# An adaLN transformer block on one core: the next unit's projection placed between the fourth and fifth up tile, with the chains, loads and stores that hang on it

## The chip, the cores and the metric

The kernel runs on one core of a Trainium2 chip. The metric is the device time of one execution in microseconds. A core has a matrix engine (TensorE, PE in the profile), a vector engine (VectorE, DVE), a scalar engine (ScalarE, ACT), GpSimd (POOL), and a queue that issues DMA transfers (SyncE, SP). Each runs its own instruction stream in order and waits for the others by semaphores.

## The reference

Eight sequences of 1024 tokens with 512 features go through one block:

```python
h = layernorm(x) * (1 + ca) + sa
x = x + ga * attention(h)                      # 16 heads, causal
h = layernorm(x) * (1 + cb) + sb
shared = relu(h @ shared_up.T)**2 @ shared_down.T          # 1024 hidden features
routed = sum over the 4 chosen of 32 experts of weight * (relu(h @ up.T)**2 @ down.T)
x = x + gb * (routed + shared)
```

The modulations (sa, ca, ga, sb, cb, gb) are computed from a small conditioning input. The router takes sigmoid(h @ gate.T), adds a bias, picks 4 of 8 groups and then 4 of 32 experts for each token, and gives every expert 256 places, filled in the order of the tokens.

## The kernel before

It has four stages: the first layernorm with the projections to q, k and v; the attention; the "ffn" stage (`project_programs`), which takes the output projection, the second layernorm, the router and the shared expert; and the 32 routed experts (`experts_programs`), which gather their tokens by index. All large products are fp32 made of three matmuls of two-part numbers (high x high, high x low, low x high): helper `exact`, L2191. So most operands exist as a pair, `_hi` and `_lo`: ScalarE or GpSimd makes the high part and VectorE or GpSimd the low part from it.

The ffn stage is where the change lies. It runs over 16 units of 512 tokens (`u = 2 * b + half`, `b` the sequence), each four token tiles (`UT = 4`, `PT = 3` is the last). Two neighbouring units overlap: while unit u goes through the shared expert, the next one is projected, normalised and transposed. Each engine has its own function `body(b, half, more)`, written out by hand, and its order of lines is the order of execution; there is no scheduler. In a middle unit:

- **TensorE**: router logits (L2251, L2253, L2254); up tiles 0 to 7 into four PSUM banks `ps_m0` to `ps_m3` (12 matmuls each), with the small matmuls that turn the logits back (L2234) after tile 0; `project` of the next unit, four tiles of 12 matmuls (`wo` times `o`); `places`, small matmuls that count places per expert (L2222 to L2225); down tiles 0 to 3, 24 matmuls each, in eight pairs of three. `turn` puts four transposes of one tile of the next unit (L2210) behind down tile 1 (tile 0), behind down tile 2 (tiles 1 and 2) and in the middle of down tile 3 (tile 3). The table `TURNS` holds that. A transpose waits for its modulated tile of `h2` and, through `lo_done`, for the low part of the tile two before it, because there are two banks `ps_t`. The first down tile waits for all eight low parts of the activations.
- **VectorE**: adds the logits (L2134); for each up tile n the low part `a_lo` (L2147), and behind the first six of them one of the steps 0 to 5 of `choose`, the router's selection; `attend` of the next unit: four times the gate sum (L145, L147, L149, and the statistics L151), the variance (L276 to L284), the reciprocal root (L290 to L298), four norms (L2025), and multiply and add of the last tile (L2032, L2034); then for each down tile the output (L2171 times gate, L2173 added to x) with the low parts of the transposed tiles (L1993) between; last `give_slots` (L2113 to L2128), which turns places into addresses. In unit 14 `give_slots` stands before `attend` and `places` before `project`.
- **ScalarE**: relu (L1965), square (L1949) and high part (L1953) of each up tile, the high part one tile later than its square; the sigmoid (L1958) behind tile 0; the root for the norm (L1930) behind tile 7; high parts of the transposed tiles (L1936).
- **GpSimd**: `modulate` of tiles 0 to 2 (L1873, L1875); `normalise` of the attention output two units ahead (L1884, L1887, L1889); 16 indirect DMAs that scatter the unit's tokens and weights to the experts' lists (`scatter`, L1912). In unit 14 four of the 16 come before `modulate`.
- **SP**: loads `o` (after the projection of the next unit, which frees its buffer), stores `h2`, stores the output (1 MB, after four tiles) and, when that has landed, loads `x` of the unit two ahead into the same buffer.

Unit 0 has the projection, the chain and its own table of choice steps behind it; unit 15 has no next unit. Ahead of the stage, the attention's end normalises and modulates unit 0 (L1253, L1259, L1266).

## Time and profile before

| | us |
|---|---|
| median of 3 runs | 2990.87 |
| lowest and highest | 2986.22, 2996.89 |
| span of the profiled execution | 3027.5 |
| TensorE busy | 2895.4 (96%) |
| VectorE busy | 2179.3 (72%) |
| ScalarE busy | 1341.6 (44%) |
| GpSimd busy | 1833.5 (61%) |

The profile is of one execution. Its page gives busy time by engine and the costliest groups of instructions; the trace behind it can be asked for the time line of an engine, for the waits (who waited, at which line, for whom, how long in all), and for the busy time and granted clock of stretches. In a time line a bracket at a row's end is the idle time before the instruction and what ended it. The ffn stage begins at 1709.0 us and ends at 2717.9 us. The gate matmul L2254 of each ffn unit marks where I cut the units: unit 1 begins at 1779.30, unit 14 at 2598.40, unit 15 at 2665.20.

### The profile page before, as it was taken

Reading aid. Unit: us, or ns where it says so; the run is one execution under the profiler, and the core shown is the slowest. Engines: PE = TensorE matmul, PEld = TensorE weight load, DVE = VectorE, ACT = ScalarE, POOL = GpSimd, SP = SyncE. Lnnn points to the kernel's source line nnn. Section 1 sums busy time; section 2 is a strip of 40 time slices with the busy share of each in tenths; the row PEclk is TensorE's granted clock in tenths of the full one; section 3 lists DMA queues with packets and bytes.
Section 4 is the critical chain, followed back from the end, with each engine's and each line's share of the span. In section 5 each row is a group of like instructions: output and inputs, shape, how many; then the busy total and the mean of one; then the engine's idle time right before and its main releaser. Section 6 shows DMA issues by size and latency. Waiting matters only on the chain.

```text
span 3027.5 us, 49806 instructions
## 1 busy us (share of the span) xinstructions
PE 2895.4 (96%) x16480; PEld 2168.3 (72%) x16480; DVE 2179.3 (72%) x5344; ACT 1341.6 (44%) x2436; POOL 1833.5 (61%) x1077
## 2 busy tenths in 40 slices
PE   8999999999999999999999989999999999989997
PEld 5788888766666666666666677777777787767775
DVE  6555555678787878787877687777777787756664
ACT  2222222156666666666666522233222333226664
POOL 1233222278888888888886256766565666655664
PEclk9999999999999999999999999999999999999998
DMA  7655555756655665566555333332322322238996
GB/s 240 211 187 201 187 180 180 233 114 136 137 124 115 138 138 121 115 139 140 119 117 160 107 97 93 94 112 74 103 79 93 102 85 81 73 107 222 239 245 118
DMA packets 281948, 420.53 MB, mean 139 GB/s; under 512 B 48463, under 2 KB 132687, under 8 KB 281742
## 3 DMA queue, kind: packets, MB, share of 16 engines
q1 hardware_dynamic: 259214, 384.22, 44.9%
q0 software_dynamic: 22528, 33.72, 5.8%
q8 instruction: 109, 1.79, 0.3%
q14 instruction: 97, 0.79, 0.1%
HBM read 263.38 MB, written 153.01 MB: 138 GB/s over the span
## 4 chain that ended last, share of the span: by engine, by line
PE 53%; DVE 14%; POOL 14%; issue 8%; ACT 4%; DMA 4%; another core or an unknown queue 2%; DVEq 1%; POOLq 0%; SPq 0%; ACTq 0%
PE qkv_ps_m L840 12%; PE ffn_ps_m L2191 11%; POOL att_gathered L1105 6%; PE qkv_ps_m L844 6%; POOL att_pt L1098 5%; PE att_ps_o L1330 5%; PE att_ps_p L1386 4%; PE att_ps_s L1304 4%; DMA out<-exp_y,exp_tok_add 2%; PE exp_ps_u L1607 2%; PE exp_ps_y L1623 1%; PE att_ps_s L1361 1%; DVE ffn_att L147 1%; DVE ffn_x L149 1%
## 5 line engine op out<-in xcount | busy, mean ns | idle before, releaser
L247 DVE CUSTOM_DVE_ANT_0 att_ps_s<-att_ps_s,att_causal 128x512 f32<-128x512 f32 (+1 forms) x992 | 469.3, 502 | 175.5 <-PE att_ps_s L1304 171.3
L1166 ACT ACTIVATE att_pt<-att_ps_p 128x512 f32<-128x512 f32 (+1 forms) x1024 | 524.5, 589 | 143.6 <-PE att_ps_p L1389 110.2
L1304 PE MATMUL att_ps_s<-att_ks,att_qs 96*128 96x512 f32 x1488 | 513.4, 373 | 2.2 <-DVE att_lower L253 0.6
L1386 PE MATMUL att_ps_p<-att_qs,att_ks 98*128 98x512 f32 (+3 forms) x1536 | 498.5, 364 | 9.3 <-ACT att_pt L1166 8.0
L1098 POOL TENSOR_TENSOR att_pt<-att_pt 128x1024 f32<-128x1024 f32 (+2 forms) x153 | 331.1, 2164 | 166.6 <-PE att_ps_o L1330 144.8
L1105 POOL TENSOR_TENSOR att_gathered<-att_gathered,att_pt 128x2048 f32<-128x2048 f32 (+1 forms) x92 | 388.1, 4218 | 7.2
L1912 POOL DMA_INDIRECT slot_info<-ffn_info,ffn_slot x256 | 275.9, 1078 | 119.3 <-issue 76.5
L253 DVE TENSOR_REDUCE att_lower<-att_ps_s 128x1 f32<-128x512 f32 x496 | 339.2, 684 | 7.4 <-PE att_ps_s L1304 7.4
L1386 PEld LDWEIGHTS att_ps_p<-att_qs,att_ks 98*128 98x128 f32 x1536 | 272.6, 191 | 82.1 <-issue 34.7
L1304 PEld LDWEIGHTS att_ps_s<-att_ks,att_qs 96*128 96x128 f32 x1488 | 275.7, 191 | 73.3 <-DVE att_rowmax L247 27.7
L577 POOL TENSOR_TENSOR qkv_x<-qkv_x,qkv_mod 128x512 f32<-128x512 f32 x60 | 83.4, 1391 | 371.5 <-DVE qkv_x L671 371.5
L1330 PE MATMUL att_ps_o<-att_pt,att_vs 128*32 128x512 f32 (+3 forms) x3072 | 267.6, 489 | 0.0
L1873 POOL TENSOR_TENSOR ffn_h<-ffn_h,ffn_mod 128x512 f32<-128x512 f32 x45 | 70.6, 1569 | 242.1 <-DVE ffn_h L2025 242.1
L2191 PE MATMUL ffn_ps_m<-ffn_dn_hi,ffn_a_hi 128*128 128x512 f32 x512 | 208.7, 408 | 5.8 <-ACT ffn_relu L1965 3.3
L2191 PE MATMUL ffn_ps_m<-ffn_hT_hi,ffn_up_hi_first 128*128 128x512 f32 x512 | 202.1, 395 | 3.8 <-issue 3.8
L1330 PEld LDWEIGHTS att_ps_o<-att_pt,att_vs 128*32 128x32 f32 x3072 | 90.1, 109 | 158.0 <-issue 117.2
L2191 PE MATMUL ffn_ps_m<-ffn_dn_hi,ffn_a_lo 128*128 128x512 f32 x512 | 203.1, 397 | 0.0
L2191 PE MATMUL ffn_ps_m<-ffn_dn_lo,ffn_a_hi 128*128 128x512 f32 x512 | 202.9, 396 | 0.0
L840 PE MATMUL qkv_ps_m<-qkv_hT_hi,qkv_w_hi 128*128 128x512 f32 x512 | 201.3, 393 | 1.4 <-DVE qkv_hT_lo L676 1.4
L2191 PE MATMUL ffn_ps_m<-ffn_hT_lo,ffn_up_hi_first 128*128 128x512 f32 x512 | 200.2, 391 | 1.1 <-issue 1.1
L840 PE MATMUL qkv_ps_m<-qkv_hT_hi,qkv_w_lo 128*128 128x512 f32 x512 | 200.5, 392 | 0.0
L2191 PE MATMUL ffn_ps_m<-ffn_hT_hi,ffn_up_lo_first 128*128 128x512 f32 x512 | 200.2, 391 | 0.2 <-issue 0.2
(311 smaller groups left out, 6718.8 us busy)
## 6 DMA issues: line engine op xcount, KB each, us to landing
att_qs<-qk_parts SPq DMA_DIRECT2D x96, 512.0 KB, 6.8
att_ks<-qk_parts SPq DMA_DIRECT2D x96, 512.0 KB, 12.7
qk_parts<-qkv_out_hi SPq DMA_DIRECT2D x128, 256.0 KB, 2.2
qk_parts<-qkv_out_lo SPq DMA_DIRECT2D x128, 256.0 KB, 2.4
qkv_x<-x SPq DMA_DIRECT2D x16, 1024.0 KB, 5.6
v_rows<-qkv_out_v SPq DMA_DIRECT2D x64, 256.0 KB, 2.3
att_vs<-v_rows SPq DMA_DIRECT2D x32, 512.0 KB, 16.1
o_parts<-att_o SPq DMA_DIRECT2D x64, 256.0 KB, 7.9
```

Of the source, the lines that this page charges most:

```text
L247: dve.tensor_tensor_reduce(part, part, self.causal[:, UNIT - (c1 - c0):UNIT], scale=1.0, scalar=MASKED, op0=ALU.add, op1=ALU.max, accum_ou ...
L253: dve.reduce_max(under[:, low:low + 1], part, axis=AX.X).then_inc(self.max_done, 1)
L840: last = pe.matmul(ps_m[n % BANKS][:, :], w_part[:, k, (n % NG) * P:(n % NG + 1) * P], h_part[:, k, :], start=k == 0 and a + c == 0, stop= ...
L844: last = pe.matmul(ps_m[n % BANKS][:, :], h_part[:, k, t * P:(t + 1) * P], (w_hi, w_lo)[c][2][:, k, :], start=k == 0 and a + c == 0, stop= ...
L1098: pool.tensor_tensor(into, into, tile(c)[:, :, col:UNIT], ALU.add).then_inc(add_done, 1)
L1105: pool.tensor_tensor(into, into, tile(c)[:, :, col:UNIT], ALU.add).then_inc(add_done, 1)
L1166: act.activation(tile(c)[:, h, col:UNIT], ps_p[(NPROB * prev.g + n) % NP][:, col:UNIT], ACT.Exp, scale=float(HD) ** -0.5).then_inc(exp_don ...
L1304: pe.matmul(bank("s", cur.g, i)[:, 0:c1 - c0], qs[cur.slot][0:STACK, h, t * P:(t + 1) * P], ks[cur.slot][0:STACK, h, c0:c1], start=True, s ...
L1330: last = pe.matmul(ps_o[h * HD:(h + 1) * HD, col:UNIT], vs[group.slot][:, kt, h * HD:(h + 1) * HD], tile(c)[:, h, col:UNIT], start=kt == 0 ...
L1386: last = pe.matmul(part[:, i * (UNIT - col):(i + 1) * (UNIT - col)], ks[prev.slot][:, h + i, kt * P:(kt + 1) * P], qs[prev.slot][:, h + i, ...
L1912: pool.indirect_dma_start(info_dram[:, :], bass.IndirectOffsetOnAxis(slot[half][:, j:j + 1].bitcast(U32), 0), info[half][:, j, :], None, b ...
L2191: last = pe.matmul(bank, a[m], c[n], start=i + j == 0, stop=i + 1 == len(pairs) and j == 2)
```

## The change

For units 1 to 14 the projection of the next unit moves from behind up tile 7 to between up tiles 3 and 4, and what hangs on it moves along: on VectorE the gate sums and the variance stand before `a_lo` 4, the reciprocal root and the norms before `a_lo` 6, and the choice steps at 0, 1, 2, 4 and 7 (the last two together); `give_slots` stands before the outputs instead of behind them. ScalarE makes the high parts 3 and 4 directly behind their squares and takes the root behind tile 4. The first down tile waits for `a_lo` pair by pair. GpSimd modulates all four tiles. Transposes 0 and 1 both stand behind down tile 1. Unit 14 loses its special order, and its scatter is one run. Outputs are stored, and x loaded, in two halves. Ahead of the stage the 12 vector operations that normalise and modulate unit 0 become 8 with two arithmetic steps in each; the rest of the diff that is left out here renumbers semaphore counts.

```diff
         PT = UT - 1
-        TURNS = ((), (0,), (1, 2), ())
-        SCATTERED_AHEAD = TOPK
+        FIRST_TURNS, TURNS = ((), (0,), (1, 2), ()), ((), (0, 1), (2,), ())
+        PAIR = UT // 2
+        AT_ONCE = (RING - 1, RING)
         CHOSEN_AHEAD, PLACED_AHEAD = {0: (0, 1), 1: (2,), 2: (3,), 3: (4, 5)}, 4
         DOWN_AT = {0: 0, 1: 1, 3: 2, 4: 3}
         FIRST_CHOICE = {1: (1,), 5: (2,), 7: (3, 4, 5)}
+        CHOICE = {0: (0,), 1: (1,), 2: (2,), 4: (3,), 7: (4, 5)}
...
+            def load_x(b, half, t0, t1):
+                src = x[bass.ds(b, 1), half * UNIT + t0 * P:half * UNIT + t1 * P, :]
+                sp.dma_start(x_sb[half][:, t0:t1, :], src.rearrange("o (t p) d -> p (o t) d", p=P)).then_inc(x_in[half], 16)
+
+            def store_out(u, half, t0, t1):
+                sp.wait_ge(out_done, CREDIT + UT * u + t1)
+                dst = out[bass.ds(u * UNIT + t0 * P, (t1 - t0) * P), :]
+                sp.dma_start(dst.rearrange("(t p) d -> p t d", p=P), x_sb[half][:, t0:t1, :]).then_inc(x_out[half], 16)
...
-                sp.wait_ge(out_done, CREDIT + UT * (u + 1))
-                dst = out[bass.ds(u * UNIT, UNIT), :]
-                sp.dma_start(dst.rearrange("(t p) d -> p t d", p=P), x_sb[half][:, :, :]).then_inc(x_out[half], 16)
-                if not (isinstance(b, int) and b == LAST):
-                    sp.wait_ge(x_out[half], CREDIT + 16 * (b + 1))
-                    load_x(b + 1, half)
+                store_out(u, half, 0, PAIR)
+                sp.wait_ge(x_out[half], CREDIT + 32 * b + 16)
+                if b < LAST:
+                    load_x(b + 1, half, 0, PAIR)
+                store_out(u, half, PAIR, UT)
+                if b < LAST:
+                    sp.wait_ge(x_out[half], CREDIT + 32 * (b + 1))
+                    sp.wait_ge(x_in[half], CREDIT + 32 * (b + 1))
+                    load_x(b + 1, half, PAIR, UT)
...
-            def modulate(b, half):
-                u = b * HALVES + half
-                for t in range(PT):
-                    pool.wait_ge(norm_done, CREDIT + UT * u + t + 1)
+            def modulate(u):
+                for t in range(UT):
+                    pool.wait_ge(norm_done, CREDIT + UT * (u - 1) + t + 1)
                     ht = h2[:, t, :]
                     pool.tensor_tensor(ht, ht, mod[:, 1, :], ALU.mult).then_inc(mul_done, 1)
-                    pool.wait_ge(mul_done, CREDIT + PT * u + t + 1)
+                    pool.wait_ge(mul_done, CREDIT + UT * u + t + 1)
                     pool.tensor_tensor(ht, ht, mod[:, 2, :], ALU.add).then_inc(h_done, 1)
...
-                if u == UNITS - 2:
-                    scatter(u, half, 0, SCATTERED_AHEAD)
                 if more:
-                    modulate(*((b, 1) if half == 0 else (b + 1, 0)))
-                if half == 0 and not (isinstance(b, int) and b == LAST) or half == 1 and more:
+                    modulate(u + 1)
+                if b < LAST:
                     normalise(u + 2)
-                scatter(u, half, SCATTERED_AHEAD if u == UNITS - 2 else 0, UT * TOPK)
+                scatter(u, half)
...
-                    if n:
+                    if n and not (u and more and n - 1 in AT_ONCE):
                         high(n - 1)
                     square(n)
                     if n == 0 and u and more:
                         scores()
                     if u == 0 and n in DOWN_AT:
                         high_weights(NW_UP + DOWN_AT[n], NW_UP + DOWN_AT[n] + 1)
+                    if u and more and n in AT_ONCE:
+                        high(n)
+                    if u and more and n == RING:
+                        root(u + 1)
                 high(UP - 1)
+                if u == 0:
+                    root(1)
                 if more:
-                    root(u + 1)
                     turn(u + 1)
...
-            def attend(b, half):
+            def gate_sums(b, half):
 
                 u = b * HALVES + half
-                own = CREDIT + LINKS * u
                 xs = x_sb[half]
-                dve.wait_ge(x_in[half], CREDIT + 16 * (b + 1))
                 dve.wait_ge(mod_in, CREDIT + 48 * (b + 2))
                 for t in range(UT):
+                    if t == 0:
+                        dve.wait_ge(x_in[half], CREDIT + (32 * b if b else 16))
+                    if t == PAIR:
+                        dve.wait_ge(x_in[half], CREDIT + 32 * b + 16)
                     last = late.gate_sum(dve, u, t, ps_m[t % RING], att, bo_sb, mod, xs, stats, LINKS * u)
                 last.then_inc(dve_own, 1)
                 late.variance(dve, LINKS * u, stats, mv, tmp)
+
+            def norms(b, half):
+
+                u = b * HALVES + half
                 late.deviation(dve, u, LINKS * u, mv, std, rstd, tmp)
-                own += 2 * UT + 1 + STAT_LINKS + ROOT_LINKS
                 dve.wait_ge(tr_done, CREDIT + UT * u)
                 dve.wait_ge(h2_out, CREDIT + 16 * u)
                 for t in range(UT):
-                    last = dve.tensor_scalar(h2[:, t, :], xs[:, t, :], mv[:, t, 0:1], rstd[:, t:t + 1],
-                                             ALU.subtract, ALU.mult)
-                    if t < PT:
-                        last.then_inc(norm_done, 1)
-
-                last.then_inc(dve_own, 1)
-                dve.wait_ge(dve_own, own + 1)
-                dve.tensor_tensor(h2[:, PT, :], h2[:, PT, :], mod[:, 1, :], ALU.mult).then_inc(dve_own, 1)
-                dve.wait_ge(dve_own, own + 2)
-                dve.tensor_tensor(h2[:, PT, :], h2[:, PT, :], mod[:, 2, :], ALU.add).then_inc(norm_done, 1)
+                    dve.tensor_scalar(h2[:, t, :], x_sb[half][:, t, :], mv[:, t, 0:1], rstd[:, t:t + 1],
+                                      ALU.subtract, ALU.mult).then_inc(norm_done, 1)
...
+                after = (b, 1) if half == 0 else (b + 1, 0)
                 for n in range(UP):
                     if u == 0 and n == 2:
                         late.last_invert(LastGroup(GROUPS - 1), 1)
+                    if u and more and n == RING:
+                        gate_sums(*after)
+                    if u and more and n == RING + 2:
+                        norms(*after)
                     if not more:
...
-                    for step in FIRST_CHOICE.get(n, ()) if u == 0 else (n,) if more else ():
+                    for step in (FIRST_CHOICE if u == 0 else CHOICE if more else {}).get(n, ()):
                         choose(u, step)
-                if u == UNITS - 2:
+                if u == 0:
+                    gate_sums(*after)
+                    norms(*after)
+                elif more:
                     give_slots(u, half)
-                if more:
-                    attend(*((b, 1) if half == 0 else (b + 1, 0)))
...
-                        for t2 in TURNS[t]:
+                        for t2 in (TURNS if u else FIRST_TURNS)[t]:
                             low_turned(u + 1, t2)
-                if u < UNITS - 2:
+                if u == 0:
                     give_slots(u, half)
...
-                if t < PT:
-                    pe.wait_ge(h_done, CREDIT + PT * u + t + 1)
-                else:
-                    pe.wait_ge(norm_done, CREDIT + UT * (u + 1))
+                pe.wait_ge(h_done, CREDIT + UT * u + t + 1)
...
+                after = (b, 1) if half == 0 else (b + 1, 0)
                 for n in range(UP):
+                    if u and more and n == RING:
+                        project(*after, lambda t: pe.wait_ge(relu_done, CREDIT + UP * u + t + 1))
                     if n < RING:
                         pe.wait_ge(fin_done, CREDIT + UT * (u - 1) + n + 1)
+                    elif u and more:
+                        pe.wait_ge(att_done, CREDIT + UT * (u + 1) + n - RING + 1)
                     else:
                         pe.wait_ge(relu_done, CREDIT + UP * u + n - RING + 1)
                     cols = slice(n * P, (n + 1) * P)
...
-                if u == UNITS - 2:
+                if first:
+                    project(*after, lambda t: pe.wait_ge(relu_done, CREDIT + UP * u + UP - RING + t + 1))
+                if more:
                     places(u)
-                if more:
-                    project(*((b, 1) if half == 0 else (b + 1, 0)), lambda t: pe.wait_ge(relu_done, CREDIT + UP * u + UP - RING + t + 1))
-                if u < UNITS - 2:
-                    places(u)
-
-                if more:
-                    pe.wait_ge(alo_done, CREDIT + UP * (u + 1))
                 if first:
+                    pe.wait_ge(alo_done, CREDIT + UP)
                     pe.wait_ge(w_lo_done, CREDIT + NW)
                 for t in range(UT):
-                    if more:
-                        pe.wait_ge(att_done, CREDIT + UT * (u + 1) + t + 1)
+                    if first:
+                        pe.wait_ge(att_done, CREDIT + UT + t + 1)
                     else:
-                        pe.wait_ge(relu_done, CREDIT + UP * (u + 1))
+                        pe.wait_ge(relu_done, CREDIT + UP * u + RING + t + 1)
                     cols = slice(t * P, (t + 1) * P)
 
                     def before_pair(n):
                         if more and t == PT and 2 * n == UP:
                             turn(u + 1, PT)
-                        if not more and t == 0:
+                        if not first and t == 0:
                             pe.wait_ge(alo_done, CREDIT + UP * u + n + 1)
 
                     exact(ps_m[t % RING][:, :], [((a_hi[:, n, cols], a_lo[:, n, cols]), (dn_hi[:, n, :], dn_lo[:, n, :]))
                                                  for n in range(UP)], before_pair).then_inc(down_done, 1)
                     if more:
-                        for t2 in TURNS[t]:
+                        for t2 in (TURNS if u else FIRST_TURNS)[t]:
```

On TensorE, in a middle unit, the order before, from the end of up tile 3 to the first down tile (within a tile one of its 12 matmuls stands for all; `wo` and `o` mark the projection, `dn` the down tiles):

```order
L2191 MATMUL ffn_ps_m3<-ffn_hT_hi,ffn_up_lo_first 128x512
L2191 MATMUL ffn_ps_m0<-ffn_hT_hi,ffn_up_hi_first 128x512
...
L2191 MATMUL ffn_ps_m3<-ffn_hT_hi,ffn_up_lo_first 128x512
L2191 MATMUL ffn_ps_m0<-ffn_wo_hi,ffn_o_hi 128x512
...
L2222 MATMUL ffn_ps_pos<-ffn_sel,ffn_before 128x32
...
L2191 MATMUL ffn_ps_m0<-ffn_dn_hi,ffn_a_hi 128x512
```

The same place now:

```order
L2194 MATMUL ffn_ps_m3<-ffn_hT_hi,ffn_up_lo_first 128x512
L2194 MATMUL ffn_ps_m0<-ffn_wo_hi,ffn_o_hi 128x512
...
L2194 MATMUL ffn_ps_m0<-ffn_hT_hi,ffn_up_hi_first 128x512
...
L2194 MATMUL ffn_ps_m3<-ffn_hT_hi,ffn_up_lo_first 128x512
L2222 MATMUL ffn_ps_pos<-ffn_sel,ffn_before 128x32
...
L2194 MATMUL ffn_ps_m0<-ffn_dn_hi,ffn_a_hi 128x512
```

The four projected tiles went ahead of the last four up tiles; `places` now directly precedes the first down tile, as before.

On VectorE, the same unit before, from the last low parts (`ffn_a_lo`) to the first output:

```order
L2147 TENSOR_TENSOR ffn_a_lo<-ffn_relu,ffn_a_hi 128x512 x2
L145 TENSOR_TENSOR ffn_att<-ffn_ps_m0,ffn_bo 128x512
...
L284 TENSOR_TENSOR ffn_mv<-ffn_tmp 128x4
L290 RECIPROCAL ffn_rstd<-ffn_std 128x4
...
L2025 TENSOR_SCALAR ffn_h2<-ffn_x0,ffn_mv,ffn_rstd 128x512 x4
L2032 TENSOR_TENSOR ffn_h2<-ffn_h2,ffn_mod 128x512
L2034 TENSOR_TENSOR ffn_h2<-ffn_h2,ffn_mod 128x512
L2171 TENSOR_TENSOR ffn_att<-ffn_ps_m0,ffn_gb 128x512
```

And now, from `a_lo` 3 on:

```order
L2149 TENSOR_TENSOR ffn_a_lo<-ffn_relu,ffn_a_hi 128x512
L145 TENSOR_TENSOR ffn_att<-ffn_ps_m0,ffn_bo 128x512
...
L284 TENSOR_TENSOR ffn_mv<-ffn_tmp 128x4
L2149 TENSOR_TENSOR ffn_a_lo<-ffn_relu,ffn_a_hi 128x512
...
L2149 TENSOR_TENSOR ffn_a_lo<-ffn_relu,ffn_a_hi 128x512
L290 RECIPROCAL ffn_rstd<-ffn_std 128x4
...
L2030 TENSOR_SCALAR ffn_h2<-ffn_x0,ffn_mv,ffn_rstd 128x512 x4
L2149 TENSOR_TENSOR ffn_a_lo<-ffn_relu,ffn_a_hi 128x512 x2
...
L2125 SCALAR_TENSOR_TENSOR ffn_slot1<-ffn_place,ffn_over 128x16
L2174 TENSOR_TENSOR ffn_att<-ffn_ps_m0,ffn_gb 128x512
```

The last two low parts stand directly behind the norms, where the last tile's multiply and add stood; the slots stand ahead of the outputs.

## Rows read from the trace of the kernel before

**Rows 1.** The page's head: busy us (share of span), instructions.

```profile
PE 2895.4 (96%) x16480; PEld 2168.3 (72%) x16480; DVE 2179.3 (72%) x5344; ACT 1341.6 (44%) x2436; POOL 1833.5 (61%) x1077
```

**Rows 2.** Length, PE busy, clock, DMA: units 1-13, 4, 8, 11, 13, 14.

```profile
1779.30:2598.40 819.10, 784.11 (x3668) 0.99 0.30 92
1966.80:2029.60 62.80, 59.57 (x283) 1.00 0.33 101
2215.60:2283.60 68.00, 62.75 (x284) 0.95 0.31 93
2415.10:2475.30 60.20, 59.44 (x284) 1.00 0.28 88
2538.10:2598.40 60.30, 59.51 (x284) 1.00 0.28 88
2598.40:2665.20 66.80, 62.68 (x283) 0.95 0.16 52
```

**Rows 3.** Waits of PE, 1709 to 2720: us, times, longest.

```profile
PE ffn_ps_t L2210 <- POOL ffn_h L1875: 26.6, 12, 5.0
PE ffn_ps_t L2210 <- DVE ffn_hT_lo L1993: 10.8, 10, 1.2
```

**Rows 4.** Time line of DVE, unit 11: start, us, instruction.

```profile
2415.18 0.68 DVE L2113 TENSOR_TENSOR ffn_picked<-ffn_onehot,ffn_ps_pos 128x512 f32<-128x512 f32 x1
...
2420.68 0.17 DVE L2128 SCALAR_TENSOR_TENSOR ffn_slot<-ffn_place,ffn_over 128x16 int32<-128x16 f32 x1
...
2431.10 0.69 DVE L2147 TENSOR_TENSOR ffn_a_lo<-ffn_relu,ffn_a_hi 128x512 fp32r<-128x512 f32 x1
...
2435.33 0.69 DVE L2147 TENSOR_TENSOR ffn_a_lo<-ffn_relu,ffn_a_hi 128x512 fp32r<-128x512 f32 x1
...
2442.43 0.69 DVE L145 TENSOR_TENSOR ffn_att<-ffn_ps_m,ffn_bo 128x512 f32<-128x512 f32 x1 [0.90 <-remote]
...
2454.82 0.18 DVE L290 RECIPROCAL ffn_rstd<-ffn_std 128x4 f32<-128x4 f32 x1 [0.27 <-ACT ffn_std L1930]
...
2455.84 3.87 DVE L2025 TENSOR_SCALAR ffn_h<-ffn_x,ffn_mv,ffn_rstd 128x512 f32<-128x512 f32 x4
```

**Rows 5.** Time line of PE, unit 11: down tile 0, seventh pair, third transpose.

```profile
2448.98 0.48 PE L2191 MATMUL ffn_ps_m<-ffn_dn_hi,ffn_a_hi 128*128 128x512 f32 x1
...
2453.18 0.39 PE L2191 MATMUL ffn_ps_m<-ffn_dn_hi,ffn_a_hi 128*128 128x512 f32 x1
...
2467.25 0.63 PE L2210 MATMUL ffn_ps_t<-all_ident,ffn_h 128*128 128x128 f32 x4 [0.76 <-DVE ffn_hT_lo L1993]
```

**Rows 6.** Time line of PE: waiting transposes of units 4 (two), 8 and 14.

```profile
2013.83 0.66 PE L2210 MATMUL ffn_ps_t<-all_ident,ffn_h 128*128 128x128 f32 x4 [2.02 <-POOL ffn_h L1875]
...
2021.59 0.63 PE L2210 MATMUL ffn_ps_t<-all_ident,ffn_h 128*128 128x128 f32 x4 [1.21 <-DVE ffn_hT_lo L1993]
...
2266.98 1.11 PE L2210 MATMUL ffn_ps_t<-all_ident,ffn_h 128*128 128x128 f32 x4 [4.37 <-POOL ffn_h L1875]
...
2647.99 1.12 PE L2210 MATMUL ffn_ps_t<-all_ident,ffn_h 128*128 128x128 f32 x4 [3.41 <-POOL ffn_h L1875]
```

**Rows 7.** DVE groups by operation, 1709 to 2720: busy us, mean ns.

```profile
L2147 DVE TENSOR_TENSOR ffn_a_lo<-ffn_relu,ffn_a_hi 128x512 fp32r<-128x512 f32 x128 | 90.1, 704 | 104.2 <-ACT ffn_a_hi L1953 73.3 <-issue 28.1
...
L2173 DVE TENSOR_TENSOR ffn_x<-ffn_x,ffn_att 128x512 f32<-128x512 f32 x64 | 56.4, 882 | 2.2
```

**Rows 8.** All instructions of L2032 in the whole trace: ns min/median/max.

```profile
L2032 DVE TENSOR_TENSOR ffn_h<-ffn_h,ffn_mod x15: 1640/1657/1664, 1763.8 to 2648.3; 128x512 f32<-128x512 f32 x15
```

**Rows 9.** Time line of POOL, unit 11: multiply and add of the first tile.

```profile
2456.47 1.51 POOL L1873 TENSOR_TENSOR ffn_h<-ffn_h,ffn_mod 128x512 f32<-128x512 f32 x1 [12.70 <-DVE ffn_h L2025]
2458.06 1.36 POOL L1875 TENSOR_TENSOR ffn_h<-ffn_h,ffn_mod 128x512 f32<-128x512 f32 x1
```

**Rows 10.** Time line of DVE ahead of the stage.

```profile
1686.12 1.92 DVE L1253 TENSOR_SCALAR ffn_h<-ffn_x,ffn_mv_first,ffn_rstd_first 128x512 f32<-128x512 f32 x4
1688.07 2.50 DVE L1259 TENSOR_TENSOR ffn_h<-ffn_h,ffn_mod_first 128x512 f32<-128x512 f32 x4
```

39 lines of the change are left out of this document (12 added, 27 removed).

## The prediction

> **What bounds the kernel now.** I read the page's head first: TensorE is busy for 96% of the span, the vector engine for 72%, GpSimd for 61% [rows 1]. In the feed-forward stage, which is where nearly all of the change lies, what counts is therefore how long TensorE stands still and at which clock it runs. Cut into its units (512 tokens each, counted from 0 to 15), the stage has three long ones among units 1 to 14 (8, 9 and 14) and eleven shorter ones; the busy time at full clock is 59.4 to 59.6 us [rows 2], and no order of the work goes below that. Units 1 to 13 together take 819.1 us, 63.0 each; the two shortest, units 11 and 13, take 60.2 and 60.3; unit 14 takes 66.8 [rows 2]. The view of waits says what the rest is: in the whole stage TensorE waits 26.6 us at the transposes for GpSimd's modulated tile and 10.8 us at the transposes for the low part of an earlier transposed tile [rows 3]. Nothing else is over 7 us.
>
> **The profiled execution against the timed ones.** The span is 3027.5 us, the median of the runs 2990.9, that is 36.6 us less. Units 1 to 13 stand 819.1 - 13 x 60.25 = 35.9 us above thirteen units like 11 and 13. The trace itself does not say which part of the program was shorter in the timed runs, but the two numbers agree so well that I take a timed unit of before to be like units 11 and 13: 60.25 us. The opposite reading is a rival below.
>
> **Why the transposes wait, and what the move does to that.** In unit 11 (its last gate matmul L2254 starts at 2415.09; I count all offsets from there) the vector engine starts the gate sums of the next unit at +27.3, has the variance at +39.5, and runs the four norms from +40.8; at the transposes only the third waits, 0.76 us [rows 4, 5]. Where the chain is some us later, as in unit 4, the first transpose waits 2.02 and the third 1.21 us [rows 6]. The change puts the projection behind the fourth up tile. Four up tiles at 12 x 0.227 = 2.72 us, with the small matmuls between, end at +12; the first projected tile is there at +14.8 instead of some +25.6 behind eight. So the norms start earlier and every transpose finds its tile. That removes the 0.76 us of unit 11 and leaves its 59.44 us of busy time [rows 2, 5].
>
> **What takes its place.** The vector engine now does the gate sums, the variance, the choice step 3 and the norms in front of the last four low parts of the activations (L2147 before, a_lo), and the first down tile waits for a_lo pair by pair. Step by step on that engine, offsets in the unit:
> - a_lo 3 began at +16.0 in unit 11 [rows 4]. The slots of the previous unit stood ahead of that chain before and do not now, so a bit earlier; I take its end, and the first gate sum, at +16.3.
> - Gate sums and variance: the engine is idle for 0.27 us ahead of the reciprocal at 2454.82, so they take 2454.55 - 2442.43 = 12.1 us [rows 4]: to +28.4.
> - a_lo 4, whose high part ScalarE now makes right behind its square, at some +27.4: 0.6 to +29.0.
> - Choice step 3, between a_lo 3 and a_lo 4 in unit 11: 2435.33 - 2431.10 - 0.61, about 3.6 us [rows 4]: to +32.6. a_lo 5: to +33.3.
> - Reciprocal to first norm, 2455.84 - 2454.82 = 1.02 us [rows 4]: to +34.4. The root's table load lies on ScalarE behind the fifth tile and is over by then.
> - Four norms, 3.87 us [rows 4]: to +38.3.
> - a_lo 6 and a_lo 7. In the trace of before all 128 of this operation average 0.704 us [rows 7]. But none of them stood where these two now stand: straight behind the norms, while GpSimd multiplies and adds on the same tiles [rows 9]. The two operations that did stand there are the last tile's multiply and add (L2032, L2034): 128x512 with two inputs in SBUF like a_lo. L2032 takes 1.64 to 1.66 us in all 15 units, with hardly any spread [rows 8], and the add is like it. The same multiply with GpSimd idle took 2.50 / 4 = 0.62 us apiece ahead of the stage [rows 10]; the norms too go from 1.92 us for four to 3.87 [rows 4, 10]. So the long time belongs to the place and not to the operation, and I price the two a_lo at 1.66 each: a_lo 6 is ready at +40.0, a_lo 7 at +41.7.
>
> TensorE's side: the first down tile began at +33.9, its seventh pair comes 2453.18 - 2448.98 = 4.2 us later [rows 5], so at +38.1. It waits there until +40.0 (1.9 us), does the pair (0.7), and waits again from +40.7 to +41.7 (1.0). Down tile 0 ends 2.9 to 3.0 us late, in every unit from 1 to 14. This wait does not exist before, where all of a_lo stands ahead of the gate sums that begin at +27.3.
>
> The Trainium skill bears on this price, page "SBUF — State Buffer", section "Who interferes with whom": a vector instruction with two SBUF inputs contends with a GpSimd instruction that reads SBUF, and whoever comes first holds the port for its whole instruction. By that rule a_lo beside GpSimd's multiplies is held up, beside its scatters not, as the rows of a_lo and of L2032 have it; by the rule the sum is the one below, 3014, and by the operation's mean alone 2986.
>
> **Behind the stall.** The vector engine goes on with choice steps 4 and 5 (some 1.8 us) and the slots (2420.85 - 2415.18, 5.7 us [rows 4]) and reaches the first output tile at about +49.5; two outputs later, at +53.4, the low part of transposed tile 0 is there. TensorE wants it at 42.4 + 5.5 + 1.3 + 5.4 = +54.6, behind down tile 2. It is ready, with a bit over 1 us to spare. GpSimd's four tiles at about 3 us each (1.51 + 1.36 and some gap [rows 9], the later ones slower) follow the norms and are done at about +48, the last of them needed at +57. GpSimd has room for the fourth tile (61% busy), and the vector engine loses the two slow operations, 3.3 us. So a unit of after is 59.44 + 2.95 = 62.4 us.
>
> **The other parts.** Unit 14: before, the scatter's first four and its slots stood ahead of the chain; its first transpose waited 3.41 us, the granted clock fell to 0.95 and it took 66.8 us [rows 2, 6]. Now it is a unit like the others: 62.4, a gain of 4.4. Unit 0 keeps its order (only the last tile's multiply and add change engine, needed long after): 0. Unit 15 gives 0: its own order stays; its scatter waits only for its own slots. x and out go in halves: the store waits for two output tiles instead of four, the x halves are wanted a unit and a half later; 0 as long as they land, and a late half would cost at most its own few us once. The SP queue's stores of h follow earlier norms. The modulation ahead of the stage (four norms in 1.92 us, four multiplies in 2.50 [rows 10], four adds alike) becomes 8 operations of 12; TensorE's attention work behind it sets when the stage begins, so 0, at most the adds' 2.5 us gained.
>
> **Sum.** Timed: 2990.9 + 13 x (62.4 - 60.25) - 4.4 = 2990.9 + 28.0 - 4.4 = 3014.5; I say 3014. In its own profile: 3027.5 - (819.1 - 811.2) - 4.4, about 3015 us, since there the units of before averaged 63.0. Bounds of the dear term: a_lo 6 and 7 at 0.70 each give a stall of 0.9 (unit 60.4), and a first gate sum that comes 2 us later makes it 5 (unit 64.4).
>
> **Rivals.**
> *Faster, because the trace's mean unit is the true one.* If timed units too are 63.0 us, as the profile has them, the stalls at the transposes and the fallen clock of units 8 and 9 (68.0 us for unit 8 [rows 2]) are real and all go. With a_lo at 1.66: -7.9 - 4.4, 2979. With a_lo at 0.70: 819.1 - 13 x 60.4 = 33.9, and 6.4 for unit 14, so 2951. For it: the waits are in the rows, and a wait of 4.37 us in unit 8 was followed by the lower clock [rows 2, 6]. Against it: the span is 36.6 us over the median and these units are the natural place for that. It decides from the point where a timed unit of before is over 62.4 us.
> *No difference.* Either a_lo 6 and 7 are not held up (unit 60.4: 2990.9 + 2 - 6.4 = 2986), or the truth of before's unit lies between, at 61.5 (+11.7 - 4.4: 2998). For it: L2173, an add with two SBUF inputs, takes 0.88 us on average [rows 7], between the two prices, so that the holding up depends on how dense GpSimd's work is.
> *Much slower.* The two new waits, 2.9 us close together, lower the granted clock. Unit 4 had 2.02 and 1.21 us and kept 1.00; unit 8 with 4.37 us and unit 14 with 3.41 us fell to 0.95, and their busy time was 62.7 instead of 59.5 [rows 2, 6]. At 3.2 us in each of 14 units: 3014 + 45 = 3059; in a third of them, 3029.
> The move does what it says: the order shows the projection ahead of the fifth up tile.
>
> **Chances.** The forecast, 3004 to 3028: 0.45. No difference, 2982 to 3000: 0.22. Faster, 2951 to 2981: 0.23. Much slower, over 3029: 0.10. A measurement of this kernel tells about 0.3% (9 us) from no change. So faster 0.23, same 0.22, slower 0.55. The range from 2968 to 3040 leaves out the lower half of the faster case and most of the clock case.
>
> **What the profile of after would show.** Right: the waits of TensorE at the transposes for GpSimd are gone; a new row, TensorE's down matmuls waiting for the vector engine's a_lo, twice a unit, with 2 to 4 us a unit or some 40 in all; the last two a_lo of a unit at about 1.66 us beside GpSimd's multiplies and the first six at 0.70; middle units near 62.4 us and as even as units 11 and 13; unit 14 like the rest. Wrong: a_lo 6 and 7 at 0.70 us; the wait under 1 us a unit; a clock of 0.95 in units that only wait for a_lo; or a new wait at the third transpose, which would say that the slots ahead of the outputs are too long.

## The result, and the profile after

The changed kernel takes 3152.4 us (median of 4 runs, 3148.5 to 3158.8) where the kernel of before takes 2988.6 us: a ratio of 1.0555, 95% interval 1.0529 to 1.0580. It is slower by 164 us. The forecast was slower by 23 us, with 3040 us as the upper end of its range. So the sign was right and the size far off.

The head of the page after (busy time, share of the span and instructions of each engine):

```profile
span 3157.1 us, 49846 instructions
PE 2959.6 (94%) x16480; PEld 2197.9 (70%) x16480; DVE 2173.7 (69%) x5310; ACT 1345.2 (43%) x2436; POOL 1846.7 (58%) x1107
```

The waits of after in the stage and behind it, of TensorE and then of ScalarE's relu (us in total, times, longest; of the transposes in [rows 3] 4.9 us for GpSimd and 2.0 us for the low part are left, and the first group below did not exist in before):

```profile
PE ffn_ps_m L2194 <- DVE ffn_a_lo L2149: 42.7, 25, 3.1
PE ffn_ps_m L2194 <- issue: 38.4, 55, 2.2
PE ffn_ps_pos L2222 <- DVE ffn_sel L2090: 21.3, 14, 3.4
PE exp_ps_t L1585 <- issue: 13.4, 1, 13.4
PE ffn_ps_t L2210 <- POOL ffn_h L1872: 4.9, 1, 4.9
...
ACT ffn_relu L1960 <- remote: 138.4, 27, 10.3
```

Units 1 to 14 of after, cut at the gate matmul as in [rows 2], and unit 6 alone (length, TensorE busy, granted clock):

```profile
1775.60:2783.60 1008.00, 905.54 (x3950) 0.94 0.26 79
2130.70:2204.00 73.30, 65.41 (x283) 0.93 0.27 87
```

A unit takes 1008.0 / 14 = 72.0 us instead of the forecast 62.4. Of unit 6's 73.3 us TensorE is idle for 7.9, and its work takes 65.4 instead of 59.4 us because the clock is down to its lower level in parts. The waits at `a_lo` are there, 42.7 us in all; that this is near the forecast's 41 is luck, as group 5 will show. Three groups are not in the forecast at all: 38.4 us of idle time, most of it in the middle of projected tiles ("issue": TensorE waited for nothing that the profile shows), 21.3 us ahead of `places`, which waits for choice step 3 (`ffn_sel`), and ScalarE's relu waiting 138.4 us for a releaser that the view calls remote: the semaphore was raised just then, but no instruction that raises it had ended shortly before.

Where the 72 us come from is best seen on the engines that wait for TensorE. ScalarE's relus of unit 6 (start, us; the bracket is the idle time before):

```profile
2134.47 0.59 ACT L1960 ACTIVATE ffn_relu<-ffn_ps_m 128x512 f32<-128x512 f32 x1
...
2137.69 0.60 ACT L1960 ACTIVATE ffn_relu<-ffn_ps_m 128x512 f32<-128x512 f32 x1 [0.34 <-PE ffn_ps_m L2194]
...
2146.87 0.60 ACT L1960 ACTIVATE ffn_relu<-ffn_ps_m 128x512 f32<-128x512 f32 x1 [7.54 <-remote]
...
2151.92 0.60 ACT L1960 ACTIVATE ffn_relu<-ffn_ps_m 128x512 f32<-128x512 f32 x1 [3.41 <-remote]
```

TensorE's rows have up tile 2 finished at 2139.95, yet its relu starts at 2146.87. The relu also waits for `a_lo` 0, but that ended at 2139.53. The trace behind the views holds the times at which semaphores were raised as well (some are missing from it). The one of up tile 2 was raised at 2146.85, that of up tile 3 at 2151.89, 6.9 and 9.2 us after the last matmul of each; ScalarE started 0.02 and 0.03 us later. So the signal of TensorE comes 7 us late, and ScalarE is not to blame. In units 1 to 14 of this profile no signal of ScalarE, VectorE or GpSimd on record came more than 0.02 us after its instruction; of TensorE's 292, 238 came within 0.02 us too, but 52 more than 0.5 us late. The chain on the vector engine starts correspondingly late. These are its first gate sum, then norms with the last two `a_lo` of the unit:

```profile
2156.09 0.68 DVE L145 TENSOR_TENSOR ffn_att<-ffn_ps_m,ffn_bo 128x512 f32<-128x512 f32 x1
...
2173.84 3.84 DVE L2030 TENSOR_SCALAR ffn_h<-ffn_x,ffn_mv,ffn_rstd 128x512 f32<-128x512 f32 x4
2177.60 3.42 DVE L2149 TENSOR_TENSOR ffn_a_lo<-ffn_relu,ffn_a_hi 128x512 fp32r<-128x512 f32 x2
```

TensorE in the same unit: one of the gaps inside a projected tile, and the matmul that waits for the last `a_lo`:

```profile
2150.38 0.39 PE L2194 MATMUL ffn_ps_m<-ffn_wo_hi,ffn_o_hi 128*128 128x512 f32 x1 [2.20 <-issue]
...
2179.40 0.79 PE L2194 MATMUL ffn_ps_m<-ffn_dn_hi,ffn_a_hi 128*128 128x512 f32 x1 [3.09 <-DVE ffn_a_lo L2149]
```

The gate sum stands at +25.4 of the unit (forecast +16.3), `a_lo` 7 ends at +50.3 (forecast +41.7). The price of the two `a_lo` beside GpSimd's multiplies is near the forecast: 3.42 us for both, 1.7 each.

### The profile page after: what moved, and what is told of

The parts are those of the page before. It is cut to its first block and busy times, and to the rows that moved or that the text cites. A ratio compares the mean times of both kernels' runs of the same rounds, so it can differ in the third digit from the quotient of the medians.

```text
span 3157.1 us, 49846 instructions
## 1 busy us (share of the span) xinstructions
PE 2959.6 (94%) x16480; PEld 2197.9 (70%) x16480; DVE 2173.7 (69%) x5310; ACT 1345.2 (43%) x2436; POOL 1846.7 (58%) x1107
## 5 line engine op out<-in xcount | busy, mean ns | idle before, releaser
L1907 POOL DMA_INDIRECT slot_info<-ffn_info,ffn_slot x256 | 257.0, 1004 | 101.5 <-issue 77.9
L1870 POOL TENSOR_TENSOR ffn_h<-ffn_h,ffn_mod 128x512 f32<-128x512 f32 x60 | 89.6, 1493 | 371.7 <-DVE ffn_h L2030 371.7
L2194 PE MATMUL ffn_ps_m<-ffn_dn_hi,ffn_a_hi 128*128 128x512 f32 x512 | 222.5, 435 | 45.8 <-DVE ffn_a_lo L2149 42.7
L2149 DVE TENSOR_TENSOR ffn_a_lo<-ffn_relu,ffn_a_hi 128x512 fp32r<-128x512 f32 x128 | 119.4, 941 | 186.5 <-issue 95.4
L2194 PE MATMUL ffn_ps_m<-ffn_dn_lo,ffn_a_hi 128*128 128x512 f32 x512 | 210.9, 412 | 0.0
L2194 PE MATMUL ffn_ps_m<-ffn_dn_hi,ffn_a_lo 128*128 128x512 f32 x512 | 210.9, 412 | 0.0
L1960 ACT ACTIVATE ffn_relu<-ffn_ps_m 128x512 f32<-128x512 f32 x128 | 75.9, 593 | 304.3 <-remote 138.4
## 6 DMA issues: line engine op xcount, KB each, us to landing
att_vs<-v_rows SPq DMA_DIRECT2D x32, 512.0 KB, 16.1
```

The source lines that it names most:

```text
L1907: pool.indirect_dma_start(info_dram[:, :], bass.IndirectOffsetOnAxis(slot[half][:, j:j + 1].bitcast(U32), 0), info[half][:, j, :], None, b ...
L2149: dve.tensor_tensor(a_lo[:, n, :], relu[n % RELU][:, :], raw(a_hi[:, n, :]), ALU.subtract).then_inc(alo_done, 1)
L2194: last = pe.matmul(bank, a[m], c[n], start=i + j == 0, stop=i + 1 == len(pairs) and j == 2)
```

## The experiments

Two theories stood at first. W: the order of the waits alone makes the 72 us. S: GpSimd's run of scatters (16 in a row in every unit) makes TensorE's signals late, and the change puts that run where the chain starts. A third came in after the first group, C: that it is a property of the chip. Runs of one group share a chip and the runs of the kernel before on it. All ratios in this table are against that kernel on the same chip:

| version | before there, us | this, us | ratio (95%) |
|---|---|---|---|
| after | 2988.6 | 3152.4 | 1.0555 (1.0529 to 1.0580) |
| group 1: after without scatters | 2966.9 | 3008.9 | 1.0145 (1.0119 to 1.0171) |
| before without scatters | 2966.9 | 2961.7 | 0.9975 (0.9960 to 0.9991) |
| after, slots last | 2966.9 | 3018.3 | 1.0177 (1.0150 to 1.0204) |
| before, slots early | 2966.9 | 3063.1 | 1.0336 (1.0307 to 1.0365) |
| group 2: before again | 2985.2 | 2982.3 | 0.9987 (0.9963 to 1.0012) |
| after again | 2985.2 | 3149.6 | 1.0556 (1.0534 to 1.0579) |
| after, norms late | 2985.2 | 3141.1 | 1.0520 (1.0491 to 1.0549) |
| after, norms late and slots last | 2985.2 | 3066.0 | 1.0295 (1.0258 to 1.0332) |
| group 3: after again | 2986.1 | 3153.6 | 1.0570 (1.0524 to 1.0616) |
| after without scatters | 2986.1 | 3004.3 | 1.0059 (1.0037 to 1.0081) |
| after, slots last | 2986.1 | 3162.1 | 1.0606 (1.0559 to 1.0653) |
| group 4: after, pauses | 2968.3 | 3023.4 | 1.0187 (1.0162 to 1.0213) |
| after, half the scatters | 2968.3 | 3000.9 | 1.0103 (1.0074 to 1.0132) |
| before, pauses | 2968.3 | 2976.4 | 1.0027 (1.0013 to 1.0040) |
| norms late, slots last, pauses | 2968.3 | 2983.1 | 1.0058 (1.0037 to 1.0079) |
| group 5: after again | 2966.6 | 3024.9 | 1.0191 (1.0170 to 1.0213) |
| after, pauses | 2966.6 | 3026.0 | 1.0185 (1.0151 to 1.0219) |
| norms late, slots last, pauses but in the last two units | 2966.6 | 2969.2 | 1.0012 (1.0001 to 1.0023) |

The five groups and the first measurement fall into two kinds of chips: one where before takes 2985 to 2989 us (the first measurement, groups 2 and 3; "late chips" from here on) and one where it takes 2967 to 2968 (groups 1, 4 and 5; "punctual chips"). Each chip was used in one group only, so a property of the chip and a condition of the hour can't be told apart; "chip" stands for both.

### Group 1: scatters taken out, slots moved

After without scatters, and the same in before:

```diff
-                for j in range(UT * TOPK):
-                    pool.indirect_dma_start(
...
+                pool.sem_inc(scattered[half], 16 * UT * TOPK)
```

> The changed kernel without its 256 scatters (GpSimd only counts the semaphore up, so the experts get no tokens of this run: their lists stay padding; the ffn stage has all its other work). Theory S: while GpSimd issues a run of scatters, TensorE's semaphores reach the other engines late (recorded: relu behind up tile 2 waits 7.5 us for one), and the change puts that run at -2 to +18 us of the unit, where the vector engine's chain starts. Then without scatters relus are punctual and the middle units of the ffn stage, cut at the gate matmul, fall from 72.4 us to 62 to 63 (the stall of 2.9 us at the first down tile stays). Theory W: the order of waits alone (a_lo behind norms, places behind choice step 3, fallen clock) makes the 72.4 us; then the units stay over 69.

> The kernel of before without its scatters (the same part left out). Theory S: no late semaphores, the middle units are 59.5 to 60.5 us instead of 60.2 to 68.6, and no transpose waits. Theory W: the units stay as they were, 63.0 on average, since the order of waits is the same.

After with `give_slots` behind the outputs, and before with it ahead of them:

```diff
-                elif more:
-                    give_slots(u, half)
+                    pass
...
-                if u == 0:
+                if more:
                     give_slots(u, half)
```

> The changed kernel with give_slots behind the outputs again, as before, and nothing else undone: the run of scatters then lies at about +7 to +29 us of a unit. Theory S: the first relus are punctual again, only semaphores from about +15 on come late (up to 4.5 us), so the gate sums start at +17 to +21 and the units take 63 to 67 us: 3020 to 3080 in all. Theory W: nothing of the chain changes but the slots' 5.7 us behind the stall, so the units stay at 70 to 73.

```diff
+                if u and u < UNITS - 2:
+                    give_slots(u, half)
                 dve.wait_ge(gb_in, CREDIT + 16 * (b + 1))
...
-                if u < UNITS - 2:
+                if u == 0:
                     give_slots(u, half)
```

> The kernel of before with give_slots ahead of the outputs in units 1 to 13 (the projection stays behind up tile 7): the run of scatters moves to the unit's beginning, as in the changed kernel. Theory S: relus of up tiles 1 to 4 come late by 4 to 9 us, up tiles 5 to 7 wait for them, and units take 62 to 68 us, 3010 to 3080 in all. Theory W: up to 2 us a unit for later outputs, 2990 to 3015.

Without scatters the units of before are 59.2 us each (unit 14 is 61.3) with TensorE hardly ever idle, and those of after 61.9 to 63.7. In total after is 47 us (1.6%) slower than before when both lack the scatters: the change without late signals. It is not yet a test of W against S, since on a punctual chip after has such units with its scatters too (group 5). Units 1 to 14 of before without scatters:

```profile
1781.00:2612.20 831.20, 829.58 (x3949) 1.00 0.29 95
```

The version with slots last took units of 62.0 to 63.9 us, near the 63 to 67 that S said and far from the 70 to 73 of W. But in none of the four profiles did a relu wait for "remote", not even in before with slots early, whose scatters start as early as in after. That speaks against S as it stood. Before with slots early is slow for another reason, on TensorE:

```profile
PE ffn_ps_t L2212 <- DVE ffn_hT_lo L1993: 65.9, 14, 6.1
```

The 5.7 us of slots delay the outputs and with them the low part of transposed tile 0; every third transpose waits up to 6.1 us, and units take 65 to 68 us. In after the slots stand at the same place and its transposes hardly wait for the low part (3.1 us in all in group 5), since its chain ends earlier. That before with slots early came out within the range that S gave is therefore luck.

### Group 2: before and after again, and the norms moved behind `a_lo` 7

```diff
-                    if u and more and n == RING + 2:
-                        norms(*after)
...
+                    if u and more and n == UP - 1:
+                        norms(*after)
                     for step in (FIRST_CHOICE if u == 0 else CHOICE if more else {}).get(n, ()):
```

> The kernel of before once more, for a profile of it on the same chip as the next three. Theory S (semaphores late because of the scatters, everywhere): relus wait for a releaser the trace calls remote, some 57 us in the stage, as in the first profile; units 60 to 68. Theory C (the lateness belongs to some chips and not to others; the runs of the last group had no remote wait and a before of 2967 instead of 2989): on a chip where before takes about 2967, no remote wait and units of 59.2 to 59.5.

> The changed kernel once more beside the others. Theory S: 1.055 of before again, units of 72, relus waiting for remote. Theory C: where before takes about 2967 the units are 62.4 to 64 (the stall at the first down tile, and the slots ahead of the outputs with some 1 us to spare), 3010 to 3040 in all; where before takes about 2990, 1.055 again.

> The changed kernel with the four norms moved behind a_lo 7, nothing else undone: no a_lo stands beside GpSimd's multiplies. Both theories: the waits for a_lo 6 and 7 are gone (30 us to under 3), so without late semaphores the units lose 2.9 us each, about 40 us in all. Theory S: with the scatters' run at the unit's start the rest of the 72.4 stays, 68 to 70 us. The slots reach the outputs at the same time as before this edit, so no new wait at the third transpose; if one comes, it is under 1 us.

> Both edits: norms behind a_lo 7 and slots behind the outputs. Expected by both theories to be the best of the order: units of 59.2 to 60 us where no semaphore is late, in unit 14 too, 2955 to 2970 and thus 0 to 10 us better than before on the same chip; where semaphores are late (before at about 2990), S and C both give 2960 to 3010, since the projection's own semaphores are then late by some 4 us.

On this chip after took 1.0556 again, with units of 71.5 to 73.7 us. Before had 11.7 us of relus waiting for remote, three times, and units of 59.2 to 59.9 but for two (67.0 and 63.5). So the first profile of before, with 63.0 us a unit, was a poor sample. Its 26.6 us of transposes waiting for GpSimd were 7.6 here and 5.4 without scatters on the punctual chip. So most of that wait, which the change was to remove, came and went with the late signals. TensorE's waits with the norms late:

```profile
PE ffn_ps_t L2210 <- DVE ffn_hT_lo L1993: 52.0, 15, 4.1
PE ffn_ps_m L2194 <- issue: 38.4, 46, 2.4
PE ffn_ps_pos L2222 <- DVE ffn_sel L2090: 21.5, 12, 2.9
```

The 43 us at `a_lo` are gone, and 52 us at the third transpose have come: norms, choice steps and slots follow each other on the vector engine, and what the norms give up in front of `a_lo` they push into the transposed tiles. The expectation of under 1 us there was wrong, and so was that of units of 68 to 70 us: they average 71.0. Only 8.5 us of the 164 came back. With slots last as well, 3066 us, where both theories had given 2960 to 3010: neither of the two waits, but "issue" with 33.0 and `ffn_sel` with 15.4 us stay. Those two do not belong to the order of norms and slots; no profile from a punctual chip or without scatters has them.

### Group 3: the same chip with and without scatters

> The changed kernel, to stand on one chip with the next two. Runs so far: on the chip where before takes 2985, after takes 1.055 of it with relus waiting for late semaphores; on the chip where before takes 2967, neither the version with slots last nor before with slots early nor those without scatters showed a late one. Theory C (only some chips are late): if before takes about 2967 here, units of 62.4 to 64 us, 1.01 to 1.025; if about 2985, 1.055. Theory S (scatters at the unit's start make them late on every chip): 1.05 or more in both cases.

> The changed kernel without its 256 scatters (the experts get no tokens), on the same chip as the one above. Theory S and the mixed one (a chip that is sensitive, and scatters that make it show): no late semaphore, units of 62 to 63.5 us on any chip. Theory C alone (the chip's TensorE signals late whatever GpSimd does): where after shows units of 72, this one is over 69 too.

> The changed kernel with give_slots behind the outputs, on the same chip as the two above. Theory S: the scatters at +7 to +29 of the unit leave the first four relus punctual; units of 62 to 67 us. On a chip where the version with norms late and slots last took 1.0295 of before, 1.03 to 1.045 (it has the a_lo stall besides); on the other kind, 1.018 again.

This group decides. It fell on a late chip: after 3153.6 us, and without its scatters 3004.3, as on a punctual one. Of the 149 us between them, 123.5 lie in units 1 to 14 (the two windows below) and the rest behind them, where the experts have no tokens to fetch. Units 1 to 14 of after on this late chip (length, TensorE busy, granted clock):

```profile
1775.10:2782.90 1007.80, 897.85 (x3949) 0.95 0.25 78
```

The same of after without scatters, on the same chip:

```profile
1772.90:2657.20 884.30, 850.65 (x3949) 0.99 0.28 89
```

Its waits: TensorE's for `a_lo`, the only large one, and all that ScalarE's relus wait for in this stage, TensorE's matmuls by their line (us in total, times), with nothing put down to remote:

```profile
PE ffn_ps_m L2191 <- DVE ffn_a_lo L2146: 29.2, 28, 1.7
```

```profile
  PE ffn_ps_m L2191: 215.4, 70
```

W is out: the order of the waits is the same in both, and the units fall from 72.0 to 63.2 us. Theory C alone is out: on the late chip nothing is late without scatters. S with position as its lever is out too: with slots last the scatters start at +3.4 and the first relus are punctual, yet the time was no better (1.0606): later relus wait 93.3 us for remote in 14 waits, and TensorE's "issue" waits grow to 60.4 us in 59. What holds is the mixed reading: on some chips, TensorE's signals are late while GpSimd issues scatters, wherever they stand.

The times at which semaphores were raised bear this out without the waits. The table counts TensorE's signals in the stage that were raised over 0.5 us after the latest matmul that could have raised them (so the lateness is at least this), by whether that matmul ended during a run of scatters, from its first to its last:

| profile | late of all, matmul ended during a run | late of all, elsewhere | longest, us |
|---|---|---|---|
| after, first profile | 53 of 91 | 2 of 238 | 9.9 |
| group 3: after | 47 of 93 | 9 of 240 | 10.0 |
| group 3: after without scatters | no runs | 0 of 364 | under 0.02 |
| group 3: after, slots last | 29 of 67 | 26 of 274 | 10.3 |
| group 2: before | 21 of 99 | 2 of 231 | 8.4 |
| group 5: after | 0 of 137 | 0 of 220 | under 0.02 |

The late ones "elsewhere" all belong to matmuls that ended within 2.1 us behind a run. In the eight profiles from late chips with scatters there are 415 late signals. Each is of a matmul that ended at least 7.1 us after the first scatter of a run, and none was raised more than 2.8 us behind the end of the last. So the first 7 us of a run are harmless, and the late signals stand in the rest of it. With slots last they are those of about +12 to +26 of the unit, the time of the projected tiles, which the change has put there.

### Group 4: pauses, and half the scatters

```diff
                         info[half][:, j, :], None, bounds_check=SLOTS - 1, oob_is_err=False).then_inc(scattered[half], 16)
+                    if j % 4 == 3:
+                        for m in range(4):
+                            pool.wait_ge(pool_own, CREDIT + 4 + 16 * u + 4 * (j // 4) + m)
+                            pool.memset(pace[:, :], 0.0).then_inc(pool_own, 1)
```

```diff
-                for j in range(UT * TOPK):
+                for j in range(UT * TOPK // 2):
```

In the second version the counts for which SyncE waits are halved too.

> The changed kernel with a pause behind every fourth scatter (four memsets of a scratch tile on GpSimd, some 2 us in all). Theory D (density: semaphores pile up only in a dense run of scatters): relus are late by under 2 us, units fall from 72 to 63 to 66 us, 3010 to 3060 on a chip where before takes about 2985. Theory N (each scatter delays, whatever its distance): lateness as before the edit, over a longer stretch, units stay at 70 to 73. Where before takes about 2967 both give about 3020.

> The changed kernel with 8 of the 16 scatters of each unit (half of the tokens' list entries are left out). Theory D: a run of 8 ends before semaphores are late by much, units 63 to 65. Theory N: half of the lateness, units 66 to 69. If position alone decided, nothing changes for the first relus.

> The kernel of before with the same pauses; its run of scatters then ends at about +37 us of a unit, ahead of the multiplies at +41. Theory D: no lateness left, 0.3 to 0.8% faster than before on a chip where before takes about 2985, the same where it takes 2967. Theory N: the same or up to 0.5% slower.

> The changed kernel with the norms behind a_lo 7, the slots behind the outputs and the pauses. Theory D: units of 59.2 to 61 us on every chip, 2950 to 2985, the best so far. Theory N: 1.02 to 1.04 of before where before takes about 2985, as without the pauses (1.0295).

The group fell on a punctual chip. There was nothing late to take away, so it stays undecided whether only dense scatters make signals late (D in the expectations) or each scatter by itself (N). Two things can be read nevertheless. Pauses cost before 0.3%: unit 14 took 66.5 us, with one transpose waiting 4.4 us for GpSimd, whose special order in that unit they delay. And in the reordered version every unit is 59.3 us. Its total was no better; TensorE waited 31.9 us at the first expert, behind the last unit's paced scatters:

```profile
2679.91 1.94 PE L1585 MATMUL exp_ps_t<-all_ident,exp_xg 128*128 128x128 f32 x8 [31.87 <-issue]
```

### Group 5: after on a punctual chip, and the best order

```diff
-                    if j % 4 == 3:
+                    if more and j % 4 == 3:
...
-                scatter(u, half)
+                scatter(u, half, b < LAST)
```

> The changed kernel on the chip of the next two. Where before takes about 2985: 1.056, units of 72. Where before takes about 2967 (mixed theory: no late semaphore there whatever the order): units of 62.7 to 63.7, 3015 to 3025, ratio 1.016 to 1.02, which is the forecast's own mechanism and size.

> The changed kernel with pauses behind every fourth scatter. Where before takes about 2985: theory D (density) 3010 to 3060; theory N (number) 3130 to 3160. Where it takes 2967: 1.019 again, 0 to 5 us more than the run above.

> Norms behind a_lo 7, slots behind the outputs, pauses in units 0 to 13 only, so that the last scatters don't hold up the experts (the paced version before it waited 31.9 us at the first expert, and its units were 59.3 us each). Where before takes 2967: 2955 to 2970. Where it takes 2985: by D 2960 to 2985, by N 3050 to 3080.

On a punctual chip after takes 3024.9 us. Its profile there has the chain that the forecast drew, but not its clock. TensorE's wait for `a_lo` in the stage, from the view of waits:

```profile
PE ffn_ps_m L2194 <- DVE ffn_a_lo L2149: 30.3, 28, 1.8
```

The time line of one unit, which starts at 2151.7: TensorE's two waits, and the vector engine's first gate sum and last two `a_lo`:

```profile
2191.26 0.50 PE L2194 MATMUL ffn_ps_m<-ffn_dn_hi,ffn_a_hi 128*128 128x512 f32 x1 [1.31 <-DVE ffn_a_lo L2149]
2192.95 0.80 PE L2194 MATMUL ffn_ps_m<-ffn_dn_hi,ffn_a_hi 128*128 128x512 f32 x1 [0.72 <-DVE ffn_a_lo L2149]
...
2167.84 0.69 DVE L145 TENSOR_TENSOR ffn_att<-ffn_ps_m,ffn_bo 128x512 f32<-128x512 f32 x1
2189.45 3.45 DVE L2149 TENSOR_TENSOR ffn_a_lo<-ffn_relu,ffn_a_hi 128x512 fp32r<-128x512 f32 x2
```

Units 1 to 14:

```profile
1772.40:2655.90 883.50, 850.05 (x3950) 0.99 0.29 90
```

28 waits, two in each of 14 units; the gate sum at +16.1 and the end of `a_lo` 7 at +41.2. The 883.5 us are those of the late chip without scatters (884.3): all that the late chip adds in these units is bound to the scatters.

Pauses alone change nothing there (3026.0 us). The best order has no idle TensorE in any unit from 1 to 14. Its window over them, and from its waits the one at the first expert:

```profile
1772.60:2602.70 830.10, 830.10 (x3950) 1.00 0.31 95
```

```profile
PE exp_ps_t L1585 <- issue: 16.0, 1, 16.0
```

It is not faster than before: 1.0012, 1.0001 to 1.0023. On a punctual chip before has little idle time in this stage to give (without scatters it loses 1.6 us in 14 units), and TensorE waits 16.0 us for the first expert. On a late chip this version was not run.

## Why the prediction was wrong

**The mechanism of the forecast was right as far as it went.** A new wait at the first down tile, caused by the norms and by GpSimd's hold on the two `a_lo` beside it, was there in every profile of the kernel after. On the punctual chip it is 30.3 us in 28 waits, 2.2 us a unit against the forecast 2.95, and the two `a_lo` take 3.45 us against 3.32. Taking the norms away from there removed it. The waits of transposes for GpSimd went, as forecast, though before itself had few of them in its later profiles. Without scatters on both sides the change cost 47 us: units 1 to 14 became 50 us longer (881.6 against 831.2), and 3 came back elsewhere. The forecast's own term, the waits at `a_lo`, is 29.1 of the 50 us; 19 are longer busy time of TensorE (848.8 against 829.6) at the lower clock, a term that the forecast's sum put at nothing and left to a rival.

**The step that failed** is the first line of the forecast's chain: "a_lo 3 began at +16.0 in unit 11 ... I take its end, and the first gate sum, at +16.3". That unit's signals are punctual at that point, and the forecast took it for granted that they would be at the new place of the scatters too. On a late chip the gate sum came at +25.4, and the end of `a_lo` 7, on which TensorE waits, at +50.3 instead of +41.7. The trace of before had shown the sign: its view of ScalarE's waits has

```profile
ACT ffn_relu L1965 <- remote: 57.1, 21, 10.9
```

The second paragraph of the prediction took whatever was above 60.25 us a unit for something that the timed runs did not have, because the two sums agreed. For the kernel of before that was right: its second profile has 59.2 to 59.9 us in most units. But the late signals did not vanish in the timed runs. In before they cost little: its gate sums come 11 us later in the unit and have slack to the transposes, and they stand at the end of the scatters, which run from +6.6 to +28.7. After puts the projection, the gate sums and all that follows from them into the time of the scatters, with no slack between, and the lateness there is larger as well: in group 2, on one chip, relus waited 11.7 us for remote in before and 150.5 us in after. The vector engine's chain ends some 9 us later in the unit shown than on the punctual chip, and the units are 8.8 us longer: 1007.8 - 884.3 = 123.5 us for 14 by the two profiles of group 3. Of this, TensorE's idle time is (1007.8 - 897.9) - (884.3 - 850.7) = 76.3 us, and 47.2 us is longer busy time, work at the lower clock.

**Mis-sized terms.** A unit of before was mostly 59.2 to 59.9 us, not 60.25. A unit of after on the punctual chip was 883.5 / 14 = 63.1, not 62.4: the waits are 0.7 us shorter than forecast, but TensorE's work takes 60.7 us instead of 59.4, since the clock falls after the waits in some units (61.4 us in the unit shown above). So this pair alone gives 3.9 us a unit instead of 2.15, and 51 us for 13 units instead of 28. It explains most of the 58 us on a punctual chip. That the 3024.9 us there lie within the forecast's 3004 to 3028 is luck: before was 24 us faster on that chip, and the change itself cost 58 us instead of 23.

**Unit 14.** It was to give 4.4 us. In the first profile it was 66.8 us, in the second 63.5, and after has it at 62.1 on the punctual chip: 1 to 5 us, as far as two profiles tell. It was also meant to have no other price, and that may not be so: before issues four scatters ahead in unit 14 and waited 11.2 us at the first expert (group 2), and in the best order TensorE waits 16.0 us there. That the four scatters make this difference was not tested; the two profiles are from different chips.

**The rivals.** "Faster" fell with its premise: the mean unit of the first profile was not the true one. "Much slower, because the clock falls" had 0.10 and priced the clock at 3.2 us a unit. The measured time is beyond it, but its mechanism is a part of the result: 20 us on a punctual chip (850.05 us busy against 830.1 in the best order), where two short waits stand before it in each unit, and 47 us more on a late one, behind a cause that it did not name. No rival had late signals as its mechanism.

**What stays open.** Why the signals are late on some chips is not settled. Nor is it why some signals of a run are late and others not. Fewer and sparser scatters were tried on punctual chips only, so whether they cure it on the others is unknown. The version with norms late and slots last keeps half of the loss and slots last alone keeps all of it; they were run on two different late chips, and the scatters lay at +7.3 to +27.5 in the one and at +3.4 to +23.6 in the other, so the two are not compared cleanly. The gaps inside a tile are not explained either, but they go with the late signals: 54 of the 55 in the first profile of after (and all 51 in group 3) fall while at least one signal of TensorE is overdue, and such times are 143 of the stage's some 1130 us. That they are the same fault seen from TensorE's side is likely by this, not shown.

## What to carry to other kernels

A wait that costs nothing in the profile of before may be slack at work. Before moving a chain forward, list the waits of every engine in the stretch into which the chain moves, those that the view can't explain above all, and price the chain with the latest of them, not with the tidiest unit. An operation's mean time says little of the place into which it is moved; take the price of whatever stood there. And measure a change on more than one chip: here the same pair of kernels gives 1.019 on one and 1.056 on another.
